# A decoder layer on one core: a re-ordered start, the weighted sums in two parts, and ScalarE work of some slots moved to GpSimd

## The chip, the cores and the metric

The kernel runs on one core of a Trainium2 chip. The metric is device time in microseconds for one execution. Three timed executions of the kernel before took 970.26, 970.6 and 971.39 us; the median is 970.6 us. The profiled execution, from which every row of the trace comes, took 968.91 us with a span of 967.1 us.

## The reference, cut to what matters

```python
x = layernorm(x + attn(x, Wq, bq, Wk, bk, Wv, bv, Wo, bo))      # x: (4, 512, 512), 16 heads of 32
x = layernorm(x + xattn(x, ctx, Wq2, bq2, Wk2, bk2))            # ctx: (4, 512, 256)
x = layernorm(x + ffn(x, w_gate, w_up, w_down))                 # 512 -> 2048 -> 512, silu(gate) * up

attn:  q, k, v = x@Wq+bq, x@Wk+bk, x@Wv+bv; rotary positions on q and k
       softmax(q k^T / sqrt(32), causal) v, for each head; then @ Wo + bo
xattn: query, key = ctx@Wq2^T+bq2, ctx@Wk2^T+bk2; x weighted by softmax(query key^T)
```

All is float32. The kernel writes each operand of a product as a rounded high part plus the rest (hi and lo, both fp32r) and adds three products: hi by hi, lo by hi, hi by lo.

## The kernel before, in words

The attention is cut into 16 groups: four batches by four groups of four heads. A group has 16 **slots**, one for each head and block of 128 query rows, in the order of rows 3, 2, 0, 1 (`ROW`). Slots are numbered through, 0 to 255, and the work ahead of the first score has negative slots from -29. Every engine runs its own loop over the same slots `t`. There is no planner: what an engine does in slot `t` stands in that loop by hand, and its instructions run in that order. An engine that waits holds back all that it has queued behind.

In slot `t` TensorE computes the scores of slot `t` into one of two PSUM banks `ps` (L675; this waits until the row maximum of slot `t - 2` is taken), then the matmuls of the *units* placed in the slot (L660), then the transposes of the probabilities of slot `t - 3` (L688). Of VectorE a slot asks for scaling, mask and row maximum (L1164), and for the copies of transposed probabilities from the banks pb and pc to `pT` (L1171, L1176). ScalarE does the exponential (L902) and the copy from bank pa (L909). When the four heads of group `n` are transposed, `weighted(n)` (L703) multiplies them with the values. It stands at the end of slot 16n + 20 (`AV`), as one block of tiled matmuls.

A **unit** is a projection or a transposition that fills one PSUM bank: `("q", n)` and `("k", n)` project group n, `("v", n)` and `("o", n)` project values and output, 12 matmuls each, three or four in a slot; `("r", n)` spreads the softmax's reciprocals, `("b", 0)` multiplies the value bias by Wo (four matmuls in plain float32). `units()` gives the first slot of each, and `ENDS` the last. A unit may start when the one before it in its bank is emptied. In the first batch there are no output projections yet, so that some slots hold scores and transposes alone: 15 to 18 and 27 to 34 among them.

**A head group's way to its scores.** ScalarE moves a projected q or k out of PSUM with its bias (`raw`, L892). VectorE swaps neighbouring rows (L1146) and multiplies by the sine (L1152). GpSimd multiplies by the cosine (L1466) and adds (L1471; for group 0 VectorE adds, L1131). ScalarE rounds to `qk_hi` (L896), and GpSimd subtracts to the rest (L1475). SP's queue stores both to `qk_scratch` in DRAM (L410, L407) and loads them back, stacked as each head needs them: `stack(n)` in slot 16n - 13 (L422), and for group 0 `first_stack` (L479, L482), which loads q whole and k in four parts, so that head 0 can start when the first part is there.

**Loads.** All go through SP's queue. At the start: the first quarter of the q and k weights, x, `w_v`, tables, the second quarter of the weights, then `ident`, `mask`, `bo`, the third quarter. The fourth quarter (512 KB) and `wo` (1024 KB) stand in slot -12, behind `first_stack`. The next batch's x is loaded in slots 10, 11, 30, 32 of each batch and split in slots 29 to 36. The fourth quarter is split by ScalarE and GpSimd in slot 8 (L865, L1500), `wo` in slots 10 to 17 (L863, L1496). `prob`, the ring of probabilities, has four places.

**The last slots.** From slot 224 the cross attention's first units (`CROSS`: c, e, t, a) stand beside the last scores; their moves are c: ScalarE moves (L936) and rounds (L941), GpSimd subtracts (L1536); e: VectorE maximum, ScalarE exponential (L946), GpSimd scales (L1542); t and a: transposes with hi on ScalarE (L952) and lo on VectorE (L1236). The first layer norm is `moments` on VectorE, `root1` on GpSimd (three short instructions, the last at L1517) and the scaling on ScalarE (L922). After slot 255 follow cross attention and the feed-forward part with no scores beside them; the change does not touch these.

Of the kernel before, what the change touches and what calls it, by code (L numbers as in the profile page):

```python
# [22 lines left out]
P = 128  # L23
# [32 lines left out]
SPLIT_W = {(1, 0): (-22, -20), (2, 0): (-8, -8)}  # L56
SPLIT_LATE = {(3, 0): 8, ("o", 0): 10, ("o", 1): 12, ("o", 2): 14, ("o", 3): 17}
LOAD_X = (10, 11, 30, 32)
# [5 lines left out]
         (("e", 3), 241, (3,), 1), (("a", 0), 243, (4,), 0), (("a", 1), 247, (4,), 0), (("a", 2), 248, (4,), 1),  # L64
# [47 lines left out]
def units():  # L112
# [6 lines left out]
    out.append((("b", 0), 11, (1, 1, 1, 1)))  # L119
    for b in range(B):  # L120
        for s in range(ST):
            out.append((("v", ST * b + s), TILES * G * b - 21 + (0, 4, 16, 20)[s], (3, 3, 3, 3)))
            out.append((("o", ST * b + s), TILES * G * b + (75, 79, 91, 95)[s], (3, 3, 3, 3)))
# [8 lines left out]
    late = {unit[0] for unit in chain}  # L132
    out = [unit + (pj_bank(unit[0], unit[1]),) for unit in out if unit[0] not in late] + CROSS + chain
# [20 lines left out]
SUMS = (ENDS["m", 4] + 17, ENDS["c", 7] + 10, ENDS["u", 5] + 2, ENDS["u", 8] + 2)  # L154

# [11 lines left out]
def program(nc, ctx, d, out):  # L167
# [93 lines left out]
    WEIGHTED = [(0, 0, 1, 6), (0, 1, 1, 8), (1, 1, 1, 9), (0, 2, 2, 0), (1, 2, 2, 2), (2, 2, 2, 4), (3, 3, 1, 7)]  # L261
# [14 lines left out]
    stored = [sem(f"stored{u}") for u in range(2)]  # L276
    stacked = [sem(f"stacked{u}") for u in range(2)]
    first_q, first_k = sem("first_q"), [sem(f"first_k{r}") for r in range(4)]
# [112 lines left out]
    def _(sp):  # L391
# [10 lines left out]
        def store(n, u, lo):  # L402

            rows = (4 * n + 2 * lo + u) * P
            if lo:
# [65 lines left out]
        def first_stack():  # L471

            for u in range(2):
                sp.wait_ge(stored[u], 32)
                for r in range(1 if u == 0 else 4):
                    for j in range(4):
                        rows = (2 * (j // 2 if u == 0 else j % 2) + u) * P
                        if u == 0:
                            sp.dma_start(qs0[D * j:D * j + D, :, :].bitcast(F32),  # L479
                                         scratch[rows:rows + P, :].rearrange("(r d) s -> d r s", d=D)).then_inc(first_q, 16)  # L480
# [12 lines left out]
        for dst, name in ((ident, "ident"), (mask, "mask"), (bo, "bo")):  # L493
            sp.dma_start(dst[:], d[name]).then_inc(late_in, 16)
        load_w(2)
        for t in range(BEGIN, END):
            for n in range(GROUPS):
                for u in range(2):
                    if t == ENDS["qk"[u], n] + SPLIT_QK:
                        store(n, u, 0)  # L500
                    if t == ENDS["qk"[u], n] + SPLIT_QK + 1:
                        store(n, u, 1)
                if t == TILES * n - 13:
# [4 lines left out]
            if t == -12:  # L508
                load_w(3)
# [1239 lines left out]
```

## Time and profile before

| what | value |
|---|---|
| three timed executions | 970.26, 970.6, 971.39 us |
| profiled execution, its span | 968.91 us, 967.1 us |
| TensorE busy with matmuls | 929.7 us (96%) |
| VectorE, GpSimd, ScalarE busy | 733.9 (76%), 598.2 (62%), 514.9 us (53%) |
| granted TensorE clock, mean | 0.994 |
| slot 0 starts, slot 20, slot 36 | 32.94, 60.16, 80.80 us |

Busy time is what an engine's instructions take; a matmul's end overlaps the start of the next. "Idle before" in a row is the time in which the engine stood still before that instruction, with the name of what released it. The distance between two starts is the cost of the one in between, and not its printed duration.

### The profile page before, as it was taken

The page shows a single profiled execution, that of the slowest core. Times are in us where ns is not written, and L with a number is a line of the kernel's source. Part 1 is how long each engine was busy: PE and PEld are TensorE (multiplying, and loading weights), DVE is VectorE, ACT ScalarE, POOL GpSimd, SP SyncE. Part 2 cuts the span into 40 slices and gives each one's busy share as a digit, 9 for nine tenths or more (in the row PEclk, how much of TensorE's full clock was granted, in tenths as well). Part 3 has the DMA queues.
Part 4 walks back from the last instruction along what each step waited for, and adds up shares of the span by engine and source line. Part 5 has one row for each costly group of instructions (what it writes and reads, how often), then busy time and mean ns, then how long its engine had stood idle before and what let it go on. Part 6 is the DMA issues. An engine that isn't in the chain of part 4 may idle for free.

```text
span 967.1 us, 16196 instructions
## 1 busy us (share of the span) xinstructions
PE 929.7 (96%) x5272; PEld 756.2 (78%) x5272; DVE 733.9 (76%) x1589; ACT 514.9 (53%) x1150; POOL 598.2 (62%) x645
## 2 busy tenths in 40 slices
PE   7888999999999978999999999999999999999997
PEld 5666888888788856887888888888878888888885
DVE  5667778678877876779478888867877888777777
ACT  4577777777877776566144443433534354333333
POOL 2467646745875546457466676777846786665644
PEclk9999999999999999999999999999999999999999
DMA  6986666965767780013102101111111113211102
GB/s 221 257 200 167 183 182 163 266 163 143 215 181 197 200 267 1 23 44 115 60 0 67 65 33 66 54 45 66 33 41 58 55 45 109 88 55 66 34 33 88
DMA packets 40883, 105.20 MB, mean 109 GB/s; under 512 B 4960, under 2 KB 5344, under 8 KB 38752
## 3 DMA queue, kind: packets, MB, share of 16 engines
q1 hardware_dynamic: 40800, 104.16, 36.7%
q8 instruction: 44, 0.72, 0.3%
q14 instruction: 39, 0.32, 0.1%
HBM read 78.98 MB, written 25.17 MB: 108 GB/s over the span
## 4 chain that ended last, share of the span: by engine, by line
PE 77%; DVE 6%; POOL 6%; ACT 5%; DMA 3%; issue 3%; SPq 0%; POOLq 0%; DVEq 0%; ACTq 0%
PE pd L712 27%; PE pj L660 14%; PE pj L712 10%; PE pg L712 5%; PE pu L712 5%; PE pv L703 3%; PE ps L675 3%; PE pa L688 2%; PE pb L688 2%; POOL raw L1466 1%; POOL raw L1475 1%; PE pc L688 1%; ACT e L946 1%; POOL raw L1471 1%; DMA qk_scratch<-raw 1%
## 5 line engine op out<-in xcount | busy, mean ns | idle before, releaser
L902 ACT ACTIVATE prob<-prob,nmax 128x512 f32<-128x512 f32 (+3 forms) x256 | 143.8, 562 | 72.9 <-DVE nmax L1164 71.8
L1164 DVE CUSTOM_DVE_ANT_0 prob<-ps,mask 128x512 f32<-128x512 f32 (+3 forms) x256 | 124.2, 487 | 72.5 <-PE ps L675 67.1
L675 PE MATMUL ps<-ks,qs 128*128 128x256 f32 (+2 forms) x256 | 104.9, 411 | 7.0 <-DVE nmax L1164 5.3
L1466 POOL TENSOR_TENSOR raw<-raw,cos 128x512 f32<-128x512 f32 x32 | 42.3, 1323 | 92.1 <-DVE pj L1146 76.5
L1633 POOL TENSOR_TENSOR g_lo<-gated,g_hi 128x512 fp32r<-128x512 f32 x32 | 46.3, 1448 | 79.7 <-ACT g_hi L1006 79.7
L1302 DVE TENSOR_TENSOR xb<-pd,xb 128x512 f32<-128x512 f32 x116 | 79.3, 684 | 19.6 <-PE pd L712 19.3
L1626 POOL TENSOR_TENSOR wop_lo<-wsum,wop_hi 128x512 fp32r<-128x512 f32 x64 | 81.6, 1299 | 1.4 <-ACT wop_hi L991 1.4
L712 PE MATMUL pd<-dn_hi,g_hi 128*128 128x512 f32 x244 | 75.4, 390 | 0.3 <-DVE x3T_lo L1250 0.3
L712 PE MATMUL pd<-dn_hi,g_lo 128*128 128x512 f32 x244 | 75.1, 389 | 0.0
L712 PE MATMUL pd<-dn_lo,g_hi 128*128 128x512 f32 x244 | 75.1, 389 | 0.0
L1606 POOL TENSOR_TENSOR wsum<-f_raw 128x256 f32<-128x256 f32 x32 | 23.7, 742 | 77.9 <-DMA f_raw<-in_w_ffn 77.7
L1006 ACT CAST g_hi<-gated 128x512 fp32r<-128x512 f32 x32 | 19.9, 622 | 91.0 <-DVE gated L1362 91.0
L991 ACT CAST wop_hi<-wsum 128x1024 fp32r<-128x1024 f32 x32 | 33.7, 1055 | 64.9 <-POOL wsum L1611 64.9
L675 PEld LDWEIGHTS ps<-ks,qs 128*128 128x128 f32 x256 | 48.8, 190 | 17.7 <-DVE nmax L1164 7.7
L660 PE MATMUL pj<-xT_hi,w_hi 128*128 128x512 f32 x128 | 51.9, 405 | 5.2 <-ACT xT_hi L872 5.1
L1475 POOL TENSOR_TENSOR raw<-raw,qk_hi 128x512 fp32r<-128x512 f32 x32 | 42.4, 1324 | 18.9 <-ACT qk_hi L896 18.9
L712 PEld LDWEIGHTS pd<-dn_hi,g_hi 128*128 128x128 f32 x244 | 45.6, 188 | 10.5 <-issue 0.7
L712 PEld LDWEIGHTS pd<-dn_hi,g_lo 128*128 128x128 f32 x244 | 45.8, 188 | 9.6
L712 PEld LDWEIGHTS pd<-dn_lo,g_hi 128*128 128x128 f32 x244 | 45.8, 188 | 9.5
L660 PE MATMUL pj<-xT_hi,w_lo 128*128 128x512 f32 x128 | 51.6, 403 | 1.5 <-DVE w_lo L1121 1.5
L660 PE MATMUL pj<-xT_lo,w_hi 128*128 128x512 f32 x128 | 51.4, 401 | 0.6 <-POOL xT_lo L1490 0.6
L688 PE MATMUL pb<-ident,prob 128*128 128x128 f32 x256 | 49.1, 274 | 0.1
(525 smaller groups left out, 2825.3 us busy)
## 6 DMA issues: line engine op xcount, KB each, us to landing
f_raw<-in_w_ffn SPq DMA_DIRECT2D x32, 768.0 KB, 4.2
qs<-qk_scratch SPq DMA_DIRECT2D x64, 256.0 KB, 4.8
ks<-qk_scratch SPq DMA_DIRECT2D x60, 256.0 KB, 7.3
qk_scratch<-qk_hi SPq DMA_DIRECT2D x32, 256.0 KB, 2.1
qk_scratch<-raw SPq DMA_DIRECT2D x32, 256.0 KB, 2.3
res<-in_x SPq DMA_DIRECT2D x4, 1024.0 KB, 5.0
x_scratch<-res SPq DMA_DIRECT2D x4, 1024.0 KB, 6.5
xb<-x_scratch SPq DMA_DIRECT2D x4, 1024.0 KB, 5.8
```

The lines of the kernel that those rows point to most:

```text
L660: mm = pe.matmul(over[at], *pairs[i], start=i == 0, stop=i == len(pairs) - 1)
L675: pe.matmul(ps[:, t % 2, 0:w], qs[n % 2][:, r, s * P:(s + 1) * P], ks[n % 2][:, r, 0:w], start=True, stop=True).then_inc(s_done, 1)
L688: mm = pe.transpose(dst[:, c:c + P], prob[:, t % PROBS, k * P:(k + 1) * P], ident[:])
L712: mm = pe.matmul(dst, stationary(k)[a], moving(k)[c], start=(first and part == 0 and k == 0), stop=(final and part == 2 and k == n - 1))
L902: act.activation(prob[:, t % PROBS, 0:w], prob[:, t % PROBS, 0:w], ACT.Exp, bias=nmax[:, n % 2, i:i + 1], scale=-1.0, accum_out=rsum[:, n ...
L991: act.copy(wop_hi[h % 2][:, 3:7, :], wsum[:]).then_inc(wophi_done, 1)
L1164: dve.tensor_tensor_reduce(prob[:, t % PROBS, 0:w], ps[:, t % 2, 0:w], mask[:, S - w:S], -D ** -0.5, 3e38, ALU.add, ALU.min, accum_out=nma ...
L1302: dve.tensor_tensor(tile, pd[:, 2 + n % 2, :], tile, ALU.add).then_inc(part_added, 1)
L1466: pool.tensor_tensor(raw[:, u, :], raw[:, u, :], cos[:], ALU.mult).then_inc(cos_done, 1)
L1475: pool.tensor_tensor(raw[:, u, :].bitcast(F32R), raw[:, u, :], qk_hi[:, u, :].bitcast(F32), ALU.subtract).then_inc(qklo_done, 1)
L1626: pool.tensor_tensor(lo[:, 3 + k:5 + k, :], wsum[:, k:k + 2, :], hi[:, 3 + k:5 + k, :], ALU.subtract).then_inc(woplo_done, 1)
L1633: pool.tensor_tensor(lo, (gated, gated_b)[b][:], hi.bitcast(F32), ALU.subtract).then_inc((glo_done, glo_b_done)[b], 1)
```

## The change

**The start.** The value units 2 and 3 move from slots -5 and -1 to 0 and 5, four matmuls a slot. The bias unit `b` moves from slot 11 to 30. The first 32 rows (head 0) of group 0's q and k go from SBUF straight to their places in `qs0` and `ks0`, eight DMAs of 64 KB issued as each part is ready, ahead of the stores; `first_stack` then loads heads 1 to 3 only. VectorE takes q and k of group 0 in one run of six instructions (swapping into free PSUM banks) in slot -21. Group 1's k is rotated 6 slots later and stored 4 slots later, and `stack(1)` stands in slot 5 for 3. The mask's zero part is written by GpSimd and 64 KB are loaded for 256. `bo` is loaded with `wo`. The fourth quarter of the weights is loaded in slot 5 and split by ScalarE and VectorE in slot 17; `wo` is loaded in slot 9 and split in slots 37 to 41; the third quarter is split in slot -11 for -8; x is loaded in slots 20, 21, 30, 31.

**The weighted sums.** `weighted_ahead(n)` stands one slot earlier than `weighted(n)` and does the products of query rows 2 and 3 with key blocks 0 and 1: 512 of the 1280 columns, which need what came from pa and pb. `weighted(n)` does the other 768, and waits for pc's copies.

**The last slots.** For batch 2 GpSimd scales the layer norm in one instruction, and ScalarE does not. For `c` 0 and 1 GpSimd rounds `cqk_hi` itself, one slot earlier than it subtracted so far. The unit `("a", 0)` moves from slot 243 to 244.

```diff
-SPLIT_W = {(1, 0): (-22, -20), (2, 0): (-8, -8)}
-SPLIT_LATE = {(3, 0): 8, ("o", 0): 10, ("o", 1): 12, ("o", 2): 14, ("o", 3): 17}
-LOAD_X = (10, 11, 30, 32)
+SPLIT_W = {(1, 0): (-22, -20), (2, 0): (-11, -11), (3, 0): (17, 17)}
+SPLIT_LATE = {("o", 0): 37, ("o", 1): 38, ("o", 2): 40, ("o", 3): 41}
+LOAD_X = (20, 21, 30, 31)
...
-    out.append((("b", 0), 11, (1, 1, 1, 1)))
+    out.append((("b", 0), 30, (1, 1, 1, 1)))
...
+    chain += [(("v", 2), 0, (4, 4, 4), 0), (("v", 3), 5, (4, 4, 4), 1)]
...
+def turned(n, u, k):
+    late = (6 if k < SPLIT_QK else 4) if (n, u) == (1, 1) else 0
+    return ENDS["qk"[u], n] + k + late
...
-    WEIGHTED = [(0, 0, 1, 6), (0, 1, 1, 8), (1, 1, 1, 9), (0, 2, 2, 0), (1, 2, 2, 2), (2, 2, 2, 4), (3, 3, 1, 7)]
+    WEIGHTED = [(0, 2, 2, 0), (1, 2, 2, 2), (2, 2, 2, 4), (3, 3, 1, 7), (0, 0, 1, 6), (0, 1, 1, 8), (1, 1, 1, 9)]
...
+            if n == 0:
+                sp.wait_ge((qkhi_done, qklo_done)[lo], u + 1)
+                for j in range(4):
+                    if lo == (j // 2 if u == 0 else j % 2):
+                        head = raw[0:D, u, :] if lo else qk_hi[0:D, u, :].bitcast(F32)
+                        sp.dma_start((qs0, ks0)[u][D * j:D * j + D, 0, :].bitcast(F32), head).then_inc((first_q, first_k)[u][0], 16)
...
-                if t == TILES * n - 13:
+                if t == TILES * n - (11 if n == 1 else 13):
...
-            if t == -12:
+            if t == 5:
                 load_w(3)
+            if t == 9:
                 load_w("o")
+                sp.dma_start(bo[:], d["bo"]).then_inc(bo_in, 16)
...
+        def weighted_ahead(n):
+            pe.wait_ge(a_moved, 4 * n + 4)
+            pe.wait_ge(b_moved, 4 * n + 4)
...
+            weighted_part(n, WEIGHTED[:2])
+        def weighted(n):
+            pe.wait_ge(c_moved, 4 * n + 4)
+            weighted_part(n, WEIGHTED[2:]).then_inc(av_done, 1)
...
+                if n == 1:
+                    act.wait_ge((first_q, first_k)[u][0], 64)
...
-                if t == hop(("o", n), 3):
+                if n // ST != 2 and t == hop(("o", n), 3):
                     layer_norm(n)
...
+            if t == ENDS["k", 0] + ROTATE:
+                swap(0, 0)
+                times_sin(0, 0)
+                swap(0, 1)
+                first_add(0)
+                times_sin(0, 1)
+                first_add(1)
...
-            if t == -7:
+            if t == 25:
                 spread_bias()
...
+            if n // ST == 2:
+                pool.tensor_scalar(res[:, s, :], res[:, s, :], mv[:, s, 0:1], rstd[:, s:s + 1], ALU.subtract, ALU.mult).then_inc(x1_done, 1)
+                return
...
+            if n < 2:
+                pool.wait_ge(cqk_moved, n + 1)
+                pool.tensor_copy(hi[:, n, :], c_raw[0][:, n, :]).then_inc(cqkhi_done, 1)
```

## Rows read from the trace of the kernel before

**Rows 1.** Windows: stretch, length, PE, PEld, DVE, ACT, POOL busy, PE clock, DMA.

```profile
100.00:300.00 200.00, 199.79 (x1579) 162.74 (x1578) 153.11 (x485) 149.96 (x414) 120.98 (x117) 1.00 0.71 187
340.00:380.00 40.00, 30.30 (x226) 22.56 (x216) 28.90 (x92) 30.75 (x85) 22.47 (x19) 0.96 0.46 154
70.00:80.00 10.00, 7.75 (x38) 5.79 (x37) 8.18 (x30) 9.30 (x26) 9.59 (x9) 0.83 0.25 65
370.00:380.00 10.00, 7.97 (x38) 5.89 (x37) 6.40 (x20) 7.20 (x20) 8.99 (x7) 0.83 0.01 3
```

**Rows 2.** Waits of PE, 10 to 60 us: us in total, times, longest.

```profile
PE pa L688 <- ACT pT L909: 2.9, 3, 1.4
PE ps L675 <- DVE nmax L1164: 2.0, 2, 1.9
PE ps L675 <- DMA ks<-qk_scratch: 1.7, 2, 1.0
PE pj L660 <- DVE w_lo L1121: 1.5, 1, 1.5
PE pj L660 <- DVE swp L1152: 1.4, 1, 1.4
```

**Rows 3.** Waits of PE, 62 to 82 us.

```profile
PE pa L688 <- ACT pT L909: 1.1, 2, 0.9
...
PE ps L675 <- DVE nmax L1164: 1.2, 2, 0.7
```

**Rows 4.** Timeline of SP's queue, 0 to 40 us: start, duration, what.

```profile
26.95 7.40 SPq L482 DMA_DIRECT2D ks<-qk_scratch  x16
```

**Rows 5.** Timeline of PE, 30 to 61 us: start, duration, instruction.

```profile
32.94 0.47 PE L675 MATMUL ps<-ks,qs 128*128 128x512 f32 x1 [0.98 <-DMA ks<-qk_scratch]
33.25 0.39 PE L660 MATMUL pj<-wv_hi,xT_hi 128*128 128x512 f32 x1
33.48 0.40 PE L660 MATMUL pj<-wv_lo,xT_hi 128*128 128x512 f32 x1
...
46.91 0.36 PE L675 MATMUL ps<-ks,qs 128*128 128x256 f32 x1
...
49.27 1.02 PE L660 MATMUL pj<-vg,rb 128*128 128x512 f32 x2
50.13 0.49 PE L688 MATMUL pb<-ident,prob 128*128 128x128 f32 x3
...
57.27 0.39 PE L675 MATMUL ps<-ks,qs 128*128 128x256 f32 x1
...
60.16 0.48 PE L675 MATMUL ps<-ks,qs 128*128 128x512 f32 x1
```

**Rows 6.** Timeline of PE, scores of slots 27, 32 and 36.

```profile
70.90 0.36 PE L675 MATMUL ps<-ks,qs 128*128 128x256 f32 x1
...
76.72 0.78 PE L675 MATMUL ps<-ks,qs 128*128 128x512 f32 x1
...
80.80 0.48 PE L675 MATMUL ps<-ks,qs 128*128 128x512 f32 x1
```

**Rows 7.** Timeline of PE, a weighted block between slots 52 and 53.

```profile
102.48 0.48 PE L675 MATMUL ps<-ks,qs 128*128 128x512 f32 x1
...
103.92 2.38 PE L703 MATMUL pv<-pT,vg 128*32 128x128 f32 x56
106.22 0.45 PE L675 MATMUL ps<-ks,qs 128*128 128x384 f32 x1
```

**Rows 8.** Timeline of DVE, 100 to 103 us.

```profile
100.81 0.69 DVE L1171 COPY pT<-pb 128x512 f32<-128x512 f32 x1
```

**Rows 9.** Waits of PE, 340 to 380 us.

```profile
PE pa L688 <- ACT pT L909: 1.8, 2, 0.9
PE pj L658 <- ACT e L946: 1.5, 1, 1.5
...
PE pj L660 <- POOL cqk_lo L1536: 0.6, 1, 0.6
```

## What I expect of the change, and why

> **What bounds the kernel now.** I read the busy shares first, then busy time by stretches, then the waits of TensorE inside the stretches that are not full, and last the timelines around each wait. TensorE is busy for 929.7 of 967.1 us. The windows show where the other 37 are: from 100 to 300 us it is busy for 199.8 of 200 us, so that there only its own work counts, and an instruction less on VectorE, ScalarE or GpSimd saves nothing. From 340 to 380 us 9.7 of 40 us are idle [rows 1]. The rest of what this change can reach lies before 82 us: from 10 to 60 us five kinds of waits add up to 2.9 + 2.0 + 1.7 + 1.5 + 1.4 = 9.5 us [rows 2], from 62 to 82 us 1.1 + 1.2 = 2.3 us [rows 3]. In both thin stretches the granted clock also falls: 0.83 over the ten us from 70 and over the ten from 370 [rows 1]. A clock at its lower level (1.2 GHz) for a third of ten us makes that mean; it costs 1.7 us of work at each place.
>
> The change adds and removes next to nothing on TensorE: the same matmuls stand in other slots. So the result is the idle time it removes, less what it adds in idle time and in changes between kinds of matmuls. I follow TensorE from station to station.
>
> **The start, slot by slot.**
>
> *To slot 0* (32.94 us before, with 0.98 us of waiting for ks just ahead [rows 5]). Value units 2 and 3 leave the slots ahead of it: 12 matmuls of one, three of the other. A matmul costs 0.23 us from start to start (33.25 to 33.48 [rows 5]), so 3.45 us of work go behind slot 0. The 1.4 us for which unit v3 waited for group 1's sine go too, since it now stands in slot 5 [rows 2]. The last 1.0 us, for ks, goes if head 0's rows land earlier. Before, these were computed, stored, and loaded back in 16 small pieces that took SP's queue 7.40 us from 26.95 [rows 4]; the first four are head 0's. Now they start from SBUF when they are made, and the run of six instructions on VectorE brings group 0's k earlier by my estimate of 3 us (a weight split of 1024 columns no longer stands between its sine and its sum). So I set slot 0 where TensorE's own work ends: 32.94 - 3.45 - 1.4 - 1.0 = 27.1. The trace has no transfer of this kind. Its price is bounded below by nothing hidden (it arrives before TensorE is through with group 1's k), above by the pieces it replaces: slot 0 would then be bound by them as before, some 4 us later at 31. I take 27.1, because the store and one way of the trip are gone from the path. The wait of 1.5 us for `w_lo` [rows 2] stays: the subtraction still stands behind group 0's rotation on VectorE. The eight DMAs cost SP's queue 8 x 0.46 (7.40 by 16 [rows 4]), 3.7 us, and four of them are taken away from `first_stack`.
>
> *Slots 0 to 10.* 46.91 - 32.94 = 14.0 us before [rows 5]. Added 3.45 us of value units; of the waits the 1.9 us (the longest wait for nmax [rows 2]) goes, because ScalarE stood there for the store of a group 1 part that competed with the late loads, and these now come in slots 5 and 9. I keep 0.4 us for head 1's part, which stands right behind in SP's queue. 14.0 + 3.45 - 1.9 + 0.4 = 15.9; slot 11 starts at 43.0, 3.9 us earlier than before.
>
> *Slots 11 to 18.* 57.27 - 46.91 = 10.4 us before [rows 5]. The bias unit leaves them: four times 0.86 us (49.27 to 50.13 [rows 5]), 3.4 us. Eight slots then hold scores and transposes alone, and TensorE no longer sets their length. What such slots cost is shown between 27 and 32: five slots in 76.72 - 70.90 = 5.8 us, 1.16 each [rows 6], with one swap and one sine on VectorE among them as here. 8 x 1.16 = 9.3. To that comes the last weight quarter in slot 17: ScalarE casts 1024 columns, VectorE waits and then subtracts, and the row maximum of slot 18 and what TensorE wants for slot 20 stand behind. That was GpSimd's before and hidden. I take 1.2 us for it; bounds are 0 (TensorE has units again in 19) and some 3 (the cast and the subtraction bare). 10.5 in all: slot 19 at 53.5. So removing 3.4 us of work saves nothing here; it is idle in its place. The rest of the waiting for copies in [rows 2] is inside these 10.5.
>
> *Slots 19 and 20.* 2.9 us before, with the longest wait for pT in it, 1.4 us [rows 2, 5]; ScalarE came late there because GpSimd was splitting `wo`. That work is now in slots 37 to 41. 1.5 us; slot 20 at 55.0 for 60.16.
>
> *Slots 20 to 36.* 80.80 - 60.16 = 20.6 us before [rows 5, 6]. The bias unit fills four bare slots: + 3.4, and the 2.3 us of waits [rows 3] and most of the 1.7 us of clock [rows 1] go, say 1.4. That would be 20.3; slots 27 to 29 stay bare, and VectorE has the spreading of the bias in slot 25 which was hidden ahead of slot 0: + 0.7. Slot 36 at 76.0: **4.8 us gained**. From there on TensorE is full as before. `wo`'s splits in slots 37 to 41 lie beside full slots; GpSimd is busy for 121 of 200 us in the full stretch [rows 1], so they are hidden at nothing; without that cover four GpSimd instructions would delay group 4's rotation, which has ten slots until it is needed.
>
> **The weighted sums.** A block takes 106.22 - 103.92 = 2.30 us [rows 7]. Its 1280 columns at the bias unit's 0.86 us for 512 (also float32) are 2.15 us, if the four narrow tiles run side by side. So 0.15 us a block is not array time, and I let it be paid twice now: 13 groups in full stretches x 0.15 = **2.0 us lost**. Bounds: 0 and 13 x 0.3. In the full stretch nothing comes back for it. TensorE must reach the early part after pb's copy: the copy ends at 100.81 + 0.69 = 101.50 [rows 8], and TensorE is there at 102.48 [rows 7], so it does not wait.
>
> The row says 0.15 us of a block are not columns. The Trainium skill, "TensorEngine Tiling (Array Packing)", section Key Properties, says that changing the tiling mode drains TensorE, and each split adds one such change in and one out. The rule gives no price; by it the loss exists, and without it the split is free here. The trace agrees with it as far as the 0.15 us go.
>
> **The last slots.** 9.7 us idle in 340 to 380 [rows 1]. What the change touches: behind group 13's block VectorE and ScalarE had nothing, and TensorE then waited 0.9 for pT; with 512 of 1280 columns a slot earlier most of that goes, 0.6. The wait for `cqk_lo`, 0.6 [rows 9], goes: GpSimd rounds at once and the rounding no longer stands behind an exponential. Unit a0 waited 1.5 us for the last exponential of an e unit [rows 9]; one slot later, with the early part of group 14 in between (0.4 x 2.3 = 0.9 us), 0.9 goes. ScalarE loses two casts and two scalings of this stretch (some 0.6 us each); where slots are bound by its row of work that gives perhaps 0.8 us. GpSimd takes them on with 22.5 of 40 us busy. I keep 0.4 back for the wait that comes next. 0.6 + 0.6 + 0.9 + 0.8 - 0.4 = **2.5 us gained**; bounds 0.5 (every wait replaced by the next) and 5.0 (with the clock's 1.7 and more).
>
> **Sum.** 4.8 - 2.0 + 2.5 = 5.3 us. The profiled execution goes from 968.9 to 963.6 us (span 961.8), and the median, which stands 1.7 us above it, from 970.6 to **965.3 us**.
>
> **Rivals.**
>
> *Everything fits better (0.20).* Slots 11 to 18 run at 1.0 us with the weight split hidden (2.5 us), the split of the sums costs nothing (2.0), and the clock's fall at 370 us stays away (1.7): 5.3 + 6.2 = 11.5, 959.1 us. For it: there is no more than one swap and one sine in eight slots. Against: the eight bare slots are the kind in which the clock fell at 70 us.
>
> *Gains at the start are eaten (0.22).* SP's queue is one, and 3.7 us of new issues stand before the stores that heads 1 to 3 need; slot 4 then waits for about 2 us, and the bare slots run at the lower clock, 1 us. Gain 2.3, 968.3 us. For it: the pieces land some four us after they are issued. Against: four fewer issues behind.
>
> *The direct transfers bring nothing (0.10).* They land no earlier than the pieces before; the start is only re-ordered, its 4.8 us vanish and the rest of the sum is 0.5: 970.1 us, no change.
>
> *The early part waits in every group (0.08), slower.* Scores of slot 20 now come 0.9 us later, between two pieces of weighted sums; VectorE and ScalarE, only two slots behind, slip, and the copy from pb misses the early part from then on. Margin 1.0 us [rows 7, 8]. With 0.75 us a group in 13 groups, 9.8 us, the time is 975.1. It decides from 0.55 us a group on (5.3 + 1.9 = 7.2 over 13). For it: in the full stretch VectorE is busy for 153 of 200 us and has little to catch up with. Against: TensorE's queue never emptied there, though a whole block of 2.30 stood in each group.
>
> **How the numbers follow.** My forecast, 962 to 968.5, has 0.40. Faster by more than 0.2% (1.9 us, about what a measurement of this kernel tells from no change) are it and the first two rivals: 0.82. Within 0.2% 0.10, slower 0.08. The range of 959 to 970.3 leaves out half of the first rival's side, and the last one.
>
> **What would show it.** Right: score 0 at about 27 us; 15.9 us from it to slot 11; slots 11 to 18 in over 9 us with TensorE waiting for nmax and pT; slot 36 at 76; a weighted group that costs over 2.30 us in its two pieces together; in 100 to 300 us no waits; under 8 us idle between slots 228 and 256. Wrong: a wait for ks or qs of more than 1 us ahead of slot 0 or 4; waits ahead of the early parts; more than the 21.7 us of before (102.48 - 80.80 [rows 6, 7]) from slot 36 to 52; the wait for `w_lo` in slot 19 over 2 us.

## The result: slower by 0.6%, where 0.5% faster was forecast

The changed kernel takes **976.65 us** (median of five runs, 974.96 to 976.95), the kernel before, on the same chip, 970.46. The ratio, with its 95% interval, is **1.0062 [1.0046, 1.0079]**: 6.0 us slower. The forecast was 965.3 us, range 959.0 to 970.3.

| | before | after |
|---|---|---|
| profiled execution, us | 968.91 | 976.65 |
| its span, us | 967.1 | 974.9 |
| mean granted clock of TensorE | 0.994 | 0.991 |
| busy in the span: TensorE, us | 929.7 | 937.4 |

TensorE is busy for 7.7 us more of a span that is 7.8 us longer, although it has the same matmuls. So the loss isn't in new idle time as a whole. It is in matmuls that take longer: because kinds of tile alternate more often, or because the clock is at its lower level. By place, the 7.8 us are 0.8 up to slot 52, 2.8 from there to slot 212, 2.4 from there to slot 255, and 1.8 behind it, where the change touches only the last weighted sum.

### The profile after

First the windows of TensorE's stretches, as in [rows 1] (columns: stretch, length, busy us of PE, PEld, DVE, ACT, POOL, then PE's granted clock, DMA share, GB/s):

```profile
100.00:300.00 200.00, 198.47 (x1551) 158.18 (x1551) 150.60 (x472) 147.69 (x408) 121.34 (x117) 1.00 0.70 187
50.00:60.00 10.00, 7.34 (x72) 4.76 (x73) 4.02 (x12) 3.73 (x10) 0.00 (x0) 0.83 0.96 267
360.00:370.00 10.00, 8.36 (x85) 5.50 (x83) 6.76 (x26) 6.87 (x18) 5.14 (x4) 0.83 0.42 172
370.00:380.00 10.00, 6.29 (x44) 4.95 (x43) 8.01 (x24) 7.84 (x23) 5.71 (x5) 1.00 0.00 1
70.00:80.00 10.00, 8.74 (x52) 5.18 (x52) 5.82 (x21) 7.48 (x22) 8.16 (x7) 1.00 0.46 156
```

From 100 to 300 us TensorE is still full but for one wait of 1.5 us. The low clock left the ten us from 70 and is now in the ten from 50. At the end it moved from 370:380 to 360:370. Two of these stretches have 0.83, as before.

TensorE's waits from 10 to 60 us (total, times, longest), which answer to [rows 2]:

```profile
PE pj L677 <- ACT w_hi L891: 2.1, 1, 2.1
PE ps L692 <- DVE nmax L1191: 1.4, 3, 0.8
PE pj L677 <- DVE w_lo L1149: 1.0, 2, 0.7
PE pa L705 <- ACT pT L937: 0.9, 1, 0.9
```

With four more of 0.6 us and less it is 7.2 us, for 9.5 before. The wait for the sine is gone and of those for ks 0.6 us are left; a new one leads, for the last quarter of the weights.

*Slot 0.* The queue of SP, with two of the four pairs that carry head 0's eight pieces (L419):

```profile
17.24 1.22 SPq L419 DMA_DIRECT2D qs<-qk_hi  x2
...
22.77 1.14 SPq L419 DMA_DIRECT2D ks<-raw  x2
```

The DMA issues by tile (last column: median us from issue to landing):

```profile
ks<-qk_scratch SPq DMA_DIRECT2D x12, 64.0 KB, 2.6
...
qs<-raw SPq DMA_DIRECT2D x2, 64.0 KB, 1.9
...
ks<-raw SPq DMA_DIRECT2D x2, 64.0 KB, 2.0
```

And TensorE's timeline, the scores of slots 0, 19, 20, 36 and 52 with what stands at the gaps between them:

```profile
25.50 0.47 PE L692 MATMUL ps<-ks,qs 128*128 128x512 f32 x1 [0.26 <-DMA ks<-raw]
...
49.49 0.38 PE L692 MATMUL ps<-ks,qs 128*128 128x256 f32 x1
51.96 0.47 PE L677 MATMUL pj<-xT_hi,w_hi 128*128 128x512 f32 x1 [2.09 <-ACT w_hi L891]
53.13 0.79 PE L677 MATMUL pj<-xT_hi,w_lo 128*128 128x512 f32 x1 [0.70 <-DVE w_lo L1149]
...
54.15 1.05 PE L705 MATMUL pa<-ident,prob 128*128 128x128 f32 x4
55.13 1.55 PE L727 MATMUL pv<-pT,vg 128*32 128x256 f32 x16
56.61 0.50 PE L692 MATMUL ps<-ks,qs 128*128 128x512 f32 x1
...
77.03 0.50 PE L677 MATMUL pj<-xT_hi,w_hi 128*128 128x512 f32 x1 [1.25 <-DVE bo L1215]
...
79.35 0.50 PE L692 MATMUL ps<-ks,qs 128*128 128x512 f32 x1
...
101.75 0.63 PE L705 MATMUL pa<-ident,prob 128*128 128x128 f32 x4 [1.53 <-ACT pT L937]
...
103.31 0.50 PE L692 MATMUL ps<-ks,qs 128*128 128x512 f32 x1
```

Three places are to be read here. **At 51.96** ScalarE's cast and then VectorE's subtraction of the last quarter of the weights had to be done, one after the other, in slot 17, two slots before the unit that needs them. After TensorE had been idle for 2.09 us and then for 0.70, its clock is at the lower level (granted 0.59 from 54.0 to 56.6 us): 1.05 us for four transposes (0.63 at 101.75) and 1.55 for the early part (1.07 at 123.70, below). **At 77.03** unit q4 waits for the bank that the moved bias unit used (the bias is added from it by VectorE). **At 101.75** TensorE waits for a copy on ScalarE, and ScalarE had waited for GpSimd:

```profile
99.20 0.62 ACT L924 CAST qk_hi<-raw 128x512 fp32r<-128x512 f32 x1 [2.48 <-POOL raw L1505]
...
101.05 0.56 ACT L937 COPY pT<-pa 128x512 f32<-128x512 f32 x1
```

GpSimd's timeline shows why it came late (L1500, L1505 and L1509 are the rotation of group 4):

```profile
85.10 1.28 POOL L1530 TENSOR_TENSOR wo_lo<-vg,wo_hi 128x512 fp32r<-128x512 f32 x1 [1.58 <-ACT wo_hi L889]
87.06 1.30 POOL L1530 TENSOR_TENSOR wo_lo<-vg,wo_hi 128x512 fp32r<-128x512 f32 x1 [0.69 <-ACT wo_hi L889]
88.32 1.30 POOL L1500 TENSOR_TENSOR raw<-raw,cos 128x512 f32<-128x512 f32 x1
89.57 1.31 POOL L1530 TENSOR_TENSOR wo_lo<-vg,wo_hi 128x512 fp32r<-128x512 f32 x1
90.81 1.31 POOL L1505 TENSOR_TENSOR raw<-raw,swp 128x512 f32<-128x512 f32 x1
92.06 1.32 POOL L1530 TENSOR_TENSOR wo_lo<-vg,wo_hi 128x512 fp32r<-128x512 f32 x1
...
97.88 1.29 POOL L1505 TENSOR_TENSOR raw<-raw,swp 128x512 f32<-128x512 f32 x1
```

From 87.06 to 99.17 us it has no gap; in the lines left out, from 93 to 97 us, are the split of an earlier group's result and two more steps of the rotation. "121 of 200 us busy" [rows 1] was true of the average and false of these 12 us. It had nothing to do from 49.9 to 64.05 us instead.

*A split group in the full stretch* (TensorE's timeline; for [rows 7]):

```profile
123.18 0.60 PE L705 MATMUL pa<-ident,prob 128*128 128x128 f32 x4
123.70 1.07 PE L727 MATMUL pv<-pT,vg 128*32 128x256 f32 x16
124.71 0.50 PE L692 MATMUL ps<-ks,qs 128*128 128x512 f32 x1
...
126.16 1.51 PE L727 MATMUL pv<-pT,vg 128*32 128x256 f32 x40
127.60 0.44 PE L692 MATMUL ps<-ks,qs 128*128 128x384 f32 x1
```

And the kernel before, transposes ahead of scores and ahead of its one block (which starts at 103.92 [rows 7]):

```profile
98.96 0.49 PE L688 MATMUL pb<-ident,prob 128*128 128x128 f32 x3
99.20 0.42 PE L675 MATMUL ps<-ks,qs 128*128 128x384 f32 x1
...
102.12 0.60 PE L688 MATMUL pa<-ident,prob 128*128 128x128 f32 x4
...
103.50 0.49 PE L688 MATMUL pb<-ident,prob 128*128 128x128 f32 x3
```

The two pieces take (124.71 - 123.70) + (127.60 - 126.16) = 2.45 us, for 2.30 in one piece: 0.15 more. The transposes ahead of a piece pay as well. Four of them take 123.70 - 123.18 = 0.52 us ahead of the early part, and 102.48 - 102.12 = 0.36 ahead of a score. The kernel before paid this once already: three transposes take 103.92 - 103.50 = 0.42 us ahead of its block, and 99.20 - 98.96 = 0.24 ahead of a score. Together that makes 0.31 us for one more piece. Whole groups agree: from the score of slot 68 to that of slot 84 it is 21.40 us, for 21.06 before. No wait stands ahead of an early part from 110 to 300 us.

*The last slots.* TensorE's waits from 340 to 382 us, for [rows 9] (this kernel is some 6 us behind there; the kernel before has the same waits for pT and nmax to 382 us as to 380):

```profile
PE pa L705 <- ACT pT L937: 2.8, 3, 0.9
PE pj L675 <- DVE att_lo L1264: 2.3, 2, 2.0
PE ps L692 <- DVE nmax L1191: 2.0, 3, 0.8
```

`cqk_lo` is gone, as is a0's 1.5 us for the last exponential. In their place stand one more wait for pT, in slot 243 where a0 had stood, and 2.0 us of **a1** for what VectorE takes from a0's bank. From slot 212 to slot 255 the windows are, before and after:

```profile
314.03:374.47 60.44, 51.75 (x433) 40.10 (x431) 47.86 (x148) 45.51 (x126) 33.18 (x33) 1.00 0.64 189
317.67:380.49 62.82, 53.26 (x418) 40.06 (x415) 48.40 (x147) 41.70 (x118) 40.34 (x35) 0.97 0.59 176
```

ScalarE has 3.8 us less to do (41.70 for 45.51) and GpSimd 7.2 us more. The lighter ScalarE shortens no wait of TensorE: in e8, with a0 in its old place, those for pT and for the exponential are the old ones.

### The profile page after: what moved, and what is told of

Read it like the earlier page. It is cut to its first block, busy times and chain, and to the rows that moved or that the text cites. A ratio compares the mean times of both kernels' runs of the same rounds, so it can differ in the third digit from the quotient of the medians.

```text
span 974.9 us, 16196 instructions
## 1 busy us (share of the span) xinstructions
PE 937.4 (96%) x5272; PEld 756.2 (78%) x5272; DVE 729.7 (75%) x1590; ACT 511.4 (52%) x1144; POOL 602.0 (62%) x647
## 4 chain that ended last, share of the span: by engine, by line
PE 79%; DVE 7%; ACT 5%; POOL 3%; issue 2%; DMA 2%; SPq 1%; POOLq 0%; DVEq 0%; ACTq 0%
PE pd L736 27%; PE pj L677 15%; PE pj L736 10%; PE pg L736 5%; PE pu L736 5%; PE pv L727 4%; PE ps L692 4%; PE pa L705 2%; PE pb L705 2%; PE pc L705 1%; ACT e L974 1%; DMA ks<-qk_scratch 1%; PE pj L675 1%; PE ps L677 1%; ACT prob L930 1%
## 5 line engine op out<-in xcount | busy, mean ns | idle before, releaser
L1500 POOL TENSOR_TENSOR raw<-raw,cos 128x512 f32<-128x512 f32 x32 | 41.3, 1293 | 89.1 <-DVE pj L1172 75.7
L1509 POOL TENSOR_TENSOR raw<-raw,qk_hi 128x512 fp32r<-128x512 f32 x32 | 42.2, 1318 | 21.8 <-ACT qk_hi L924 21.7
L736 PEld LDWEIGHTS pd<-dn_hi,g_hi 128*128 128x128 f32 x244 | 45.6, 188 | 10.5 <-issue 0.7
```

Source lines behind the costliest of these rows:

```text
L736: mm = pe.matmul(dst, stationary(k)[a], moving(k)[c], start=(first and part == 0 and k == 0), stop=(final and part == 2 and k == n - 1))
L1500: pool.tensor_tensor(raw[:, u, :], raw[:, u, :], cos[:], ALU.mult).then_inc(cos_done, 1)
L1509: pool.tensor_tensor(raw[:, u, :].bitcast(F32R), raw[:, u, :], qk_hi[:, u, :].bitcast(F32), ALU.subtract).then_inc(qklo_done, 1)
```

## Experiments

Each is named by its label. Ratios are to the kernel before on the same chip; 0.001 is 0.97 us. The starts of scores in each kernel's one profiled execution, in us:

| slot | before | after | e1 | e2 | e3 | e5 | e6 | e7 | e9 | e11 |
|---|---|---|---|---|---|---|---|---|---|---|
| 0 | 32.94 | 25.50 | 25.61 | 33.03 | 25.85 | 26.07 | 25.49 | 26.12 | 25.91 | 25.53 |
| 11 | 46.91 | 42.01 | 42.20 | 48.53 | 42.65 | 42.41 | 42.15 | 42.78 | 39.44 | 42.24 |
| 19 | 57.27 | 49.49 | 50.49 | 59.80 | 51.01 | 50.75 | 50.28 | 50.75 | 50.44 | 50.64 |
| 20 | 60.16 | 56.61 | 55.63 | 62.96 | 55.39 | 58.07 | 55.46 | 53.61 | 52.92 | 53.88 |
| 36 | 80.80 | 79.35 | 79.23 | 83.94 | 78.14 | 82.29 | 79.72 | 76.64 | 75.92 | 78.56 |
| 52 | 102.48 | 103.31 | 102.83 | 105.48 | 102.07 | 104.29 | 103.34 | 97.68 | 96.97 | 101.22 |
| 212 | 314.03 | 317.67 | 313.93 | 319.83 | 316.41 | 318.65 | 314.38 | 308.76 | 308.12 | 315.57 |

In kernels with split sums the score of slot 20 stands behind an early part. That shifts it by 1.0 to 1.5 us against the others, and the rest of the block comes later.

The two last stretches of the same executions, with TensorE's granted clock:

| | before | after | e1 | e2 | e3 | e4 | e5 | e6 | e7 | e8 | e9 | e10 | e11 | e12 |
|---|---|---|---|---|---|---|---|---|---|---|---|---|---|---|
| slot 212 to 255, us | 60.44 | 62.82 | 60.67 | 60.14 | 63.82 | 62.74 | 63.73 | 61.52 | 60.18 | 61.04 | 61.50 | 62.33 | 61.75 | 61.31 |
| clock in it | 1.00 | 0.97 | 1.00 | 1.00 | 0.92 | 0.97 | 0.95 | 0.97 | 1.00 | 0.97 | 0.97 | 0.95 | 0.97 | 0.97 |
| slot 255 to the end, us | 592.6 | 594.4 | 591.6 | 592.7 | 593.0 | 592.7 | 592.9 | 591.6 | 593.4 | 591.6 | 591.6 | 592.8 | 592.4 | 592.7 |
| clock in its first 10 us | 0.83 | 0.83 | 1.00 | 0.83 | 1.00 | 0.83 | 0.83 | 1.00 | 0.83 | 1.00 | 1.00 | 1.00 | 0.83 | 0.83 |
| clock 70 to 80 us behind slot 255 | 1.00 | 0.83 | 1.00 | 1.00 | 0.83 | 1.00 | 1.00 | 1.00 | 1.00 | 1.00 | 1.00 | 0.83 | 1.00 | 1.00 |

Behind slot 255 all these kernels do the same but for the last weighted sum, and yet they differ by up to 2.8 us: 591.6 us where the clock stays up in both places, 592.4 to 593.4 with one fall, 594.4 with both, in the changed kernel. Ahead of it every execution of 61 us and more has a fall in it, and none of the four under 61. So a single profile can't show a gain or a loss of one or two us in these stretches; the ratios, from several executions each, decide.

**The three parts, taken apart**

*e1_sums_whole*: the changed kernel, with the early part in the same slot as the rest.

```diff
-                if t == (TILES * n + AV if n < GROUPS - 1 else LAST_AV) - 1:
+                if t == (TILES * n + AV if n < GROUPS - 1 else LAST_AV):
```

> The changed kernel with the two pieces of each weighted sum next to each other again, in the later slot; the same products in the same order, all else as changed. My theory: a piece of its own costs 0.28 us in each full group (21.40 against 21.06 us from slot 68 to slot 84), 16 groups, so this is 4.5 us faster than the changed kernel: about 972.2 us. Rival (the longer groups come from VectorE and ScalarE being pushed out of step by the earlier piece, and a slip once made stays): 6 us or more faster, and the waits before slot 100 shrink too. Third: the extra length is elsewhere, and this stays at 976.6.

968.14 us, ratio 0.9987 [0.9975, 0.9998]. Without the split the change isn't slower, but a little faster than the kernel before. These are 7.3 us less than the changed kernel, more than the split costs by itself (e2, e11).

*e2_split_alone*: the kernel before, with the split and the new order of `WEIGHTED` alone.

```diff
+                if t == (TILES * n + AV if n < GROUPS - 1 else LAST_AV) - 1:
+                    weighted_ahead(n)
```

> The kernel before with nothing changed but the weighted sums in two parts. My theory: 0.28 us for each of 14 groups lost, and up to 1 us won back where TensorE idles (slots 19, 35, 227, 243): 970.5 + 3.3 = 973.8 us, and 21.35 us from slot to slot 16 later in the full stretch. Rival (two pieces let VectorE and ScalarE run closer, which the thin stretches at both ends turn into time): 968 to 970 us. If the loss only arises with the new start, it is within 970 to 971.

974.2 us, ratio 1.0045 [1.0029, 1.0061]: 4.4 us lost. The full stretch has no idle time at all:

```profile
100.00:300.00 200.00, 200.00 (x1538) 159.56 (x1540) 151.57 (x479) 149.17 (x410) 121.75 (x118) 1.00 0.70 186
```

Its ten groups from slot 52 to 212 take 214.35 us, as in the changed kernel (214.36), and 2.8 more than the 211.55 before. In the seven other kernels with whole sums they take 211.03 to 211.15; the profiled execution of the kernel before has one group 0.45 us longer, with a wait for `xT_lo` at 256.13. Against these seven a split group costs 0.33 us. So the loss is TensorE's own time. (Of the 3.0 us by which its slot 52 is late, 1.6 come before slot 4, where nothing differs but the granted clock of that one execution: 0.66 from 34 to 38 us.)

*e4_late_alone*: the kernel before, with the changes of the last slots alone.

```diff
-         (("e", 3), 241, (3,), 1), (("a", 0), 243, (4,), 0),
+         (("e", 3), 241, (3,), 1), (("a", 0), 244, (4,), 0),
...
-                if t == hop(("o", n), 3):
+                if n // ST != 2 and t == hop(("o", n), 3):
...
-                if key[0] == "c" and t == hop(key, 1):
+                if key[0] == "c" and key[1] >= 2 and t == hop(key, 1):
...
+            if n // ST == 2:
+                pool.tensor_scalar(res[:, s, :], res[:, s, :], mv[:, s, 0:1], rstd[:, s:s + 1], ALU.subtract, ALU.mult).then_inc(x1_done, 1)
+                return
...
+            if n < 2:
+                pool.wait_ge(cqk_moved, n + 1)
+                pool.tensor_copy(hi[:, n, :], c_raw[0][:, n, :]).then_inc(cqkhi_done, 1)
```

> The kernel before with the changes of the last slots alone (layer norm of batch 2 and the rounding of c 0 and 1 on GpSimd, unit a0 in slot 244). My theory after the result: a0 a slot later passes its wait on to a1 and to the next copies (2.0 us for att_lo at slot 247, against 1.5 at 243 before), and the relief of ScalarE is off the path: 970.0 to 971.5 us. Rival A (my forecast's): 968.0 us. Rival B (it costs what slots 212 to 255 lost, 2.4 us less two splits): 972.3 us.

971.24 us, ratio 1.0009 [0.9997, 1.0021]. The 2.5 us of the forecast aren't there; a loss of 0.9 can't be told from none. Its waits from 340 to 382 us are those of the changed kernel:

```profile
PE pa L688 <- ACT pT L909: 2.8, 3, 0.9
PE pj L658 <- DVE att_lo L1236: 2.4, 2, 2.0
```

*e8_late_a0_back*: the same, with `("a", 0)` at 243 again.

> The kernel before with the changes of the last slots, but unit a0 in slot 243 as before. My theory: a0 and a1 share a bank and stand three slots apart after the change, so that a1 waits 2.0 us for a0's lo part; with a0 back this goes, and what GpSimd took from ScalarE stays a gain of 1 to 1.5 us by slot 244: 969.3 us, against 971.2 with a0 moved. Rival (the 2 us are the lower clock or ScalarE's own row, whatever a0 does): 971 us again.

969.56 us, ratio 0.9996 [0.9984, 1.0007]. Its waits over the same stretch:

```profile
PE pa L688 <- ACT pT L909: 1.8, 2, 0.9
PE pj L658 <- ACT e L946: 1.5, 1, 1.5
```

The third wait for pT and the 2.0 us for `att_lo` go, and the 1.5 us of [rows 9] are back: they follow a0's place. What it leaves (rounding and scaling on GpSimd) is worth nothing that can be measured (0.4 us by the ratio).

*e6_start_alone*: the changed kernel with the sums whole and the last slots undone, so the new start alone.

> The changed start on the kernel before: sums whole, last slots as before. My theory: slots 36 on stand 1.6 us ahead, 52 on 0.3 us behind (as with the sums whole before), and slots 212 to 255 cost what they cost before, 60.4 us: 970 to 970.5 us, no gain. Rival (the late part is harmless and the start alone is worth its 2 us): 968 us, as the changed kernel with whole sums.

969.35 us, ratio 0.9997 [0.9986, 1.0007], where the forecast had 4.8 us of gain for this part. Slot 0 is 7.4 us ahead, slot 52 is 0.9 us behind.

*e10_split_and_late*: the kernel before with the split and the last slots.

> The kernel before with the sums in two parts and the last slots' changes, and not the new start. Alone they cost 3.9 and 0.9 us. My theory: they add, 975.2 us, and what the whole change loses beyond the sum of its three parts (976.6 against 970.4 + 3.9 + 0.9 - 1.0 = 974.2) comes from the new start with the split. Rival (the early part of group 14 and the moved a0 meet in slots 243 to 247 and pull the clock down there): 977 us or more.

975.55 us, ratio 1.0056 [1.0042, 1.0071]; e2 and e4 added give 1.0054. So the two do not help each other, and the early part does not fill the new wait for pT: it is 0.92 us in slot 243 here, as in e4.

The three parts add up to +4.4 + 0.9 - 0.3 = 5.0 us, for 6.0 measured with an interval of 4.5 to 7.7 us.

**Where the start's gain went**

*e3_w3_apart*: the changed kernel; ScalarE casts the last quarter of the weights in slot 15, VectorE subtracts in slot 17.

```diff
-SPLIT_W = {(1, 0): (-22, -20), (2, 0): (-11, -11), (3, 0): (17, 17)}
+SPLIT_W = {(1, 0): (-22, -20), (2, 0): (-11, -11), (3, 0): (15, 17)}
```

> The changed kernel with ScalarE casting the last weight quarter in slot 15 and VectorE subtracting in 17, for both in 17. My theory: VectorE stood idle for the cast in slot 17 (2.4 us), TensorE waited 2.1 + 0.7 us for the weights and then ran at the lower clock; all but 0.7 us of it goes, and slot 20 starts at 53.5 for 56.6: 976.6 - 3 = 973.6 us. Rival (the load of these weights itself lands late, since it is issued behind the stack of group 1 and with wo): the wait stays, now of ScalarE in slot 15, and the time is 976 to 978.

972.42 us, ratio 1.0028 [1.0015, 1.0041], by the ratios 3.3 us better than the changed kernel. The wait for `w_hi` is gone. Slots 19 to 20 take 4.38 us for 7.12; in this execution the clock was low already from 48 us on (0.50 from 48 to 52), so its profile shows less than the runs do.

*e5_wo_early*: the changed kernel; `wo` is split in slots 20 to 23, where GpSimd was idle.

```diff
-SPLIT_LATE = {("o", 0): 37, ("o", 1): 38, ("o", 2): 40, ("o", 3): 41}
+SPLIT_LATE = {("o", 0): 20, ("o", 1): 21, ("o", 2): 22, ("o", 3): 23}
```

> The changed kernel with the output weights split in slots 20 to 23, where GpSimd stood idle for 14 us, for slots 37 to 41. My theory: four GpSimd subtractions beside group 4's rotation made its k late, ScalarE waited 2.5 us for it and TensorE 1.5; slots 36 to 52 then take 22.1 us for 23.96, and the time is 976.6 - 1.8 = 974.8 us. Rival (the next batch's x comes late from its loads and is the cause): no change of slots 36 to 52, 976 to 977 us.

976.26 us, ratio 1.0068 [1.0054, 1.0081]: no gain, and yet it did its own part. Slots 36 to 52 take 22.0 us for 23.96, and the wait of 1.53 us at 101.75 is not there. The two us were lost before slot 36, where the wait for the weights remains and the clock of the profiled execution is low for the whole of eight us:

```profile
50.00:58.00 8.00, 5.78 (x27) 3.19 (x27) 3.22 (x11) 3.92 (x10) 0.32 (x1) 0.50 0.87 283
```

The new start alone (e6), which splits `wo` late, has 0.50 in the same window, so the early `wo` isn't the cause of that. Why the median gained nothing is open; its six executions have the lowest mean clock of all kernels, 0.988 (see "What stays open").

*e7_start_mended*: e6 with three things put right at once: the weights' cast two slots before the subtraction, `wo` early, and the bias unit at 28, so that q4 no longer stands behind it.

```diff
-SPLIT_W = {(1, 0): (-22, -20), (2, 0): (-11, -11), (3, 0): (17, 17)}
-SPLIT_LATE = {("o", 0): 37, ("o", 1): 38, ("o", 2): 40, ("o", 3): 41}
+SPLIT_W = {(1, 0): (-22, -20), (2, 0): (-11, -11), (3, 0): (15, 17)}
+SPLIT_LATE = {("o", 0): 20, ("o", 1): 21, ("o", 2): 22, ("o", 3): 23}
...
-    out.append((("b", 0), 30, (1, 1, 1, 1)))
+    out.append((("b", 0), 28, (1, 1, 1, 1)))
```

> The changed start alone with three repairs: last weight quarter cast in slot 15 and subtracted in 17, output weights split in slots 20 to 23, bias unit in slot 28 for 30. My theory: the start's own gain of 6 to 7 us at slot 0 then survives to slot 52, less what slots 11 to 18 lose: repairs give 0.9 (weights) + 1.8 (output weights) + 1.2 (bias unit's bank) on the start alone, 966 to 967 us. Rival (slots 11 to 18 and 27 hold too little for TensorE, so that every repair only turns into waiting elsewhere and the clock falls): 969 us or more.

**964.95 us, ratio 0.9956 [0.994, 0.9971]**: 4.3 us faster than before. TensorE's waits from 42 to 82 us:

```profile
PE pa L705 <- ACT pT L937: 2.4, 3, 1.3
PE ps L692 <- DVE nmax L1191: 1.9, 4, 0.8
```

`w_hi` (2.1) and `bo` (1.3) are gone; what remains is the round through VectorE and ScalarE in slots that have no other work. Slot 52 is at 97.68, 4.8 us ahead of the kernel before: the size that the forecast gave the start. Three edits went in together, so how the 4.0 us between e6 and e7 divide is known by the gaps of the trace, not by runs of each.

*e11_mended_split*: e7 with the split sums.

> The mended start with the weighted sums in two parts. My theory: a fixed price for each further entry into the narrow tiles, 0.28 us in 14 full groups, whatever the start: 965.0 + 3.9 = 968.9 us. Rival (with the new start it costs twice that, as 968.1 against 976.6 us showed): 973 us.

969.41 us, ratio 1.0003 [0.9989, 1.0016]. Against e7 4.5 us lost, as 4.4 in e2: on the good start as on the old one, the split costs the same. From slot 52 to 212 it takes 214.35 us, for 211.08 in e7.

**Can the empty slots be filled?**

*e9_v3_later*: e7, with value unit 3 in slots 13 to 16, three matmuls each, instead of from slot 5.

```diff
-    chain += [(("v", 2), 0, (4, 4, 4), 0), (("v", 3), 5, (4, 4, 4), 1)]
+    chain += [(("v", 2), 0, (4, 4, 4), 0), (("v", 3), 13, (3, 3, 3, 3), 1)]
```

> The mended start with value unit v3 in slots 13 to 16, three matmuls a slot, for slots 5 to 7. My theory: slots 5 and 6 hold seven matmuls each and bind TensorE, while 11 to 18 hold none and leave it idle (2 us of waits and a lower clock); moving 2.7 us of work from there to here hides it: 965.0 - 2.5 = 962.5 us, and no fall of the clock at slot 16. Rival (the thin slots are bound by a ring of latencies between VectorE, ScalarE and TensorE, into which units put their own length): 965 us.

965.45 us, ratio **0.9944 [0.9932, 0.9956]**, which can't be told from e7; 2.5 us of gain were expected. Slot 11 comes 3.3 us earlier, at 39.44, but slot 19 only 0.3. TensorE's waits from 16 to 110 us:

```profile
PE ps L692 <- DMA ks<-qk_scratch: 2.0, 1, 2.0
PE pa L705 <- ACT pT L937: 1.7, 3, 1.3
PE pj L677 <- DVE swp L1178: 1.4, 1, 1.4
```

Slots 11 to 18 take 11.00 us, for 7.97 in e7. Of the 3.0 us, 2.8 are v3's own twelve matmuls (0.23 each), and the waits did not shrink for them: TensorE waits 3.6 us in these slots, for 2.2 in e7. v3 waits 1.4 us for its bank, which holds group 1's k until VectorE has multiplied it by the sine, and slot 16 waits 2.0 us for the rows of that k from memory. It starts at 48.07; in e7, where v3 was done before, at 48.34 without that wait. So v3 in slots 5 to 7 had been filling time in which the k was on its way. The granted clock is 1.00 from 40 to 60 us here, 0.83 in e7.

*e12_v3_and_late*: e9 with the last slots of the change, a0 at 243.

> The mended start with v3 in slots 13 to 16 and the last slots' changes with a0 kept in slot 243. My theory: the late part is worth 0 to 1 us (969.6 against 970.4 on the kernel before), 962 us if v3 does what I expect. Rival (relief of ScalarE in the last slots is off the path): the same as without it.

966.44 us, ratio 0.9952 [0.9939, 0.9965]: nothing added, as e8 said.

## Why the prediction was wrong, step by step

The sum was 4.8 for the start, - 2.0 for the split, + 2.5 for the last slots. In runs of their own the three are worth + 0.3, - 4.4 and - 0.9 us, the first and the last no more than noise. So all three terms failed, and the sign of the whole with them. The split's mechanism was right and its price less than half of the real one. At the start and in the last slots the work did move as planned, and new waits took the gain.

**Slot 0: right, a little small.** 27.1 forecast, 25.50 measured, with TensorE's own work in front of it and 0.26 us of waiting. Of the two bounds for the direct transfer the lower one held: each landed about 2.0 us after its issue. SP's eight issues took 0.58 us each (1.14 to 1.22 for two), for the 0.46 assumed, and harmed nobody.

**Slots 0 to 10 and 11 to 18: 15.9 and 10.5 us forecast, 16.5 and 7.5 measured** (42.01 - 25.50 and 49.49 - 42.01). Together 24.0 for 26.4. Bare slots cost less than the 1.16 us of the row they were priced from: 0.94. That they would take over 9 us was one of my signs for "right", and it failed. The 1.2 us for the weights were put here and weren't paid here: TensorE ran ahead to slot 19 and stood there.

**Slots 19 to 20: failed.** 1.5 us forecast, 7.12 measured. 2.09 + 0.70 us are the hand-over of the weights. The bound of "some 3 (the cast and the subtraction bare)" was right (1.04 + 1.22 us), but I took 1.2 of it, because units would cover it in slot 19. The unit in slot 19 is the one that needs these weights. (A wait of over 2 us there was my own sign for "wrong".) That TensorE then works at 1.2 GHz until about 56.6 us was not in the sum, nor that the early part, 1.5 us at that clock, now stands ahead of slot 20. e3 took away the wait and gained 3.3 us.

**Slots 20 to 36: 21.0 us forecast, 22.74 measured.** 1.25 of the 1.7 is q4's wait for the bias unit's bank. I priced the moved unit by its columns and didn't ask who has its bank next. Of the 2.3 us of old waits that were to go, 1.0 is still there, for nmax at 69.75; from 62 to 82 us the waits add up to 2.3 as before. The clock in 70:80 is back at 1.00, as forecast.

**`wo`'s splits in slots 37 to 41, "hidden at nothing": failed.** From slot 36 to 52 it took 23.96 us for 21.68 before. This was my own sign for "wrong". The sentence that named the price of lost cover ("would delay group 4's rotation, which has ten slots until it is needed") had the mechanism and dismissed it. Two of the four subtractions of 1.3 us stand ahead of the rotation on the same engine and came late themselves, because ScalarE had not cast yet; two stand between its steps, of q and of k. The unit that waits isn't the one that needs the k, but ScalarE's own cast of it at 99.20, with TensorE's copy behind it in ScalarE's queue. e5 took 2.0 us from these slots with this change alone.

**The split sums: right in kind, 2.0 us forecast, 4.4 measured.** The mis-sized term is the 0.15 us a group. In the full stretch a group costs 0.33 us more (0.28 against the one profile of the kernel before), above the upper bound of 0.3; for 13 groups that is 4.3 us. The 0.15 that one block has beyond its columns is what its two pieces show together (2.45 for 2.30). Left out were the transposes just ahead of a piece, which take 0.16 to 0.18 us longer than ahead of a score. The trace of the kernel before had this number (0.42 for 0.24), outside the rows that I priced from. "In the full stretch nothing comes back for it" held. The rule of the Trainium skill ("TensorEngine Tiling (Array Packing)", Key Properties: changing the mode drains TensorE) agrees with the sign in four pairs of kernels (before and e2, e7 and e11, e4 and e10, e1 and the changed kernel). The page has no price.

**The last slots: 2.5 us gained by forecast, 0.9 lost in e4, nothing in e8.** Of the four terms only `cqk_lo` went as said. The term of 0.9 us for a0 failed: moved one slot, it is three slots from a1 instead of four, and a1 needs the same bank; a1 paid 2.0 where a0 had paid 1.5. The term of 0.6 for pT failed: the wait in slot 231, behind group 13's block, is 0.92 us with the split as without it, and another 0.92 came in slot 243. The 0.8 for ScalarE's lighter row failed too: with 3.8 us less to do there it let nothing start earlier. From slot 228 to 255 TensorE is idle for 9.2 us, for 8.7 before; under 8 was my sign for "right".

**Which rival it was.** None in full. "Gains at the start are eaten" had the right effect (e6: 0.3 us of gain left) by the wrong mechanism: neither slot 4 nor SP's queue waited. "The early part waits in every group" was my only way to be slower; it is refuted by the full stretch without waits. The slower outcome came from the sum of the split, twice my price, and a start and an end that brought nothing. A sum of small new waits that cancels the gains was no rival of mine.

**What stays open.** e1 (0.9987) is 1.8 us better than start and last slots added (1.0006), so that the split seems to cost 7.3 us on the changed kernel and 4.4 to 4.6 elsewhere (e2, e11 against e7, e10 against e4); and e5 is no better than the changed kernel though its slots 36 to 52 are. No run separated these. What the record shows is that the clock differs between executions by as much. From 34 to 38 us it is 0.66 in e2, 0.65 in e4 and 1.00 in e8, whose work there is that of the kernel before, and behind slot 255 a second fall goes with the 1.8 us named above. All timed executions of the kernel before, 69 beside the experiments, say the same: the 19 with a mean granted clock of 0.996 took 968.8 us on average, the 15 with 0.991 took 970.8. The mean is 0.993 over these 69, 0.992 in e1, 0.991 in e6, 0.990 in the changed kernel and 0.988 in e5. My estimate from these two groups, 0.4 us for 0.001, puts 1.3 us of the changed kernel's loss and 1.9 us of e5's down to the clock. Whether these kernels bring the lower clock about, by their waits, or met it by chance isn't shown.

## What to carry to other kernels

A split that one engine casts and another subtracts costs both durations in a row in the slot where it is due. Put the second two slots after the first, and look up which unit reads the result before calling it covered. When a unit moves, follow its bank and not its columns: the next user of that bank inherits the wait. An engine with 40% idle over a stretch can still be full in the twelve us in which it carries a chain that others need; read its timeline there. Before a block is split, look at what stands ahead of it too: here half the price of one more change of tiles lay in the transposes before the block.

## What the runs showed of the hardware that I had not expected

- A transfer of 64 KB from SBUF to SBUF landed 1.9 to 2.0 us after its issue. The pieces through memory (`ks<-qk_scratch`) landed 2.6 us after theirs (3.6 in the kernel before), and those had a store before them. The new way takes no longer than one leg of the old one.
- One more entry into tiles of 128x32 in float32 costs TensorE 0.33 us (211.08 us in e7 and 214.35 in e11 for ten groups). About half of it, 0.15, lies in the blocks themselves, and the other half in the transposes just ahead of them.
- In bare slots, with no single wait over 1.3 us, the clock still fell to 1.2 GHz: 0.80 from 42 to 50 us and 0.77 from 50 to 58 in e7. With v3 in these slots (e9) it was at 1.00, and the time the same.
- Behind slot 255 fourteen profiled executions took 591.6 to 594.4 us with the same instructions but for the last weighted sum, in the order of how often the clock fell there. This spread is nearly half of what the whole change was measured to cost.
